# Weight chunks loaded one ahead, and a tile's loads issued before an older store, in a recurrent attention and FP4 feed-forward kernel

## The reference

```python
xn = layernorm(x)
# branch s: linear attention with phi(t) = exp(-t*t/2), 16 heads, then an MLP
q, k, v = rmsnorm(xn) @ qkv_w.T             # q, k -> phi(q), phi(k)
out = (phi(q) @ (phi(k).T @ v)) * z         # z: reciprocal of phi(q) @ sum(phi(k))
x2 = xn + gamma * (out @ proj_w.T + proj_b)
s = x2 + gamma * (gelu(rmsnorm(x2) @ conv1_w.T + conv1_b) @ conv2_w.T + conv2_b)
# branch g: feed-forward in which both operands of each product are quantized
gate = fq(xn) @ fq(w_gate).T                # w_gate, w_up: 2816 x 1024
up   = fq(xn) @ fq(w_up).T
h = silu(gate) * up
g = silu(fq(h) @ fq(w_down).T)              # w_down: 1024 x 2816
out = x + s * g
```

## Time and profile before

| | us |
|---|---|
| three runs | 7118.3, 7091.09, 7113.65 |
| their median | 7113.65 |
| the profiled execution | 7141.09 |
| its span on the slowest core (core 0) | 7139.5 |
| busy: VectorE (DVE) | 3880.3 |
| busy: TensorE matmul (PE) | 2700.8 |
| busy: ScalarE (ACT) | 2051.6 |
| busy: TensorE weight load (PEld) | 1144.1 |

### The profile page before, as it was taken

How to read it: one execution, slowest core, us unless ns; L and a number is a source line. 1 busy time by engine, 2 the same in 40 slices (tenths; PEclk the granted TensorE clock), 3 DMA queues, 4 the chain that set the end, 5 groups by cost and what they waited for, 6 DMA issues and landing times.

```text
span 7139.5 us, 58299 instructions; the slowest of 8 cores (7062.0 to 7139.5 us)
## 1 busy us (share of the span) xinstructions
PE 2700.8 (38%) x10905; PEld 1144.1 (16%) x11098; DVE 3880.3 (54%) x8760; ACT 2051.6 (29%) x4067; POOL 3.2 (0%) x13
## 2 busy tenths in 40 slices
PE   0066446643214033375003555522222322222299
PEld 0022122211101011132001222211111111111043
DVE  0500330033676866524886777667777777777522
ACT  0133223321222222221223333323333333333211
POOL 0000000000000000000000000000000000000000
PEclk9988678866556566677556667755555555555598
DMA  8500010013111110000113222221101110111254
GB/s 100 144 22 24 31 46 23 19 40 77 36 40 34 37 35 32 31 24 26 49 37 93 88 88 88 84 64 41 41 28 41 41 40 29 41 41 41 71 177 172
DMA packets 227699, 396.08 MB, mean 55 GB/s; under 512 B 147861, under 2 KB 147989, under 8 KB 217626
## 3 DMA queue, kind: packets, MB, share of 16 engines
q1 hardware_dynamic: 226778, 375.57, 16.2%
q0 software_dynamic: 576, 16.78, 2.1%
HBM read 246.44 MB, written 145.33 MB: 55 GB/s over the span
## 4 chain that ended last, share of the span: by engine, by line
PE 31%; issue 25%; DVE 20%; ACT 12%; DMA 6%; SPq 5%; DVEq 1%; ACTq 0%
PE ups L1121 5%; PE gps L1067 5%; PE kvg_ps L394 4%; PE d_ps L1219 4%; PE c1ps L911 3%; SPq L195 2%; PE c2ps L939 2%; DMA xqu<-xqT_h 2%; PE q_ps L443 2%; PE prA L588 2%; DVE gld L1133 1%; DMA winw<-L_ffn_w_up 1%; PE xp4t L1153 1%; DMA winw<-L_ffn_w_gate 1%; DMA xa<-x 1%
## 5 line engine op out<-in xcount | busy, mean ns | idle before, releaser
L1153 PE MATMUL xp4t<-ident_b,hq 128*128 128x128 bf16 x704 | 179.1, 262 | 1308.4 <-ACT hqf L1159 1259.9
L1121 PE MATMUL ups<-wquT,xqu 128*128 128x512 bf16 (+1 forms) x1504 | 381.8, 424 | 240.8 <-DMA xqu<-xqT_h 207.6
L363 DVE SCALAR_TENSOR_TENSOR xn<-xn,rstd_all,rep_s 128x1024 bf16<-128x1024 f32 x32 | 41.1, 1285 | 689.7 <-ACT xn L352 689.7
L1133 DVE TENSOR_TENSOR gld<-gld,up 128x2816 f32<-128x2816 f32 x32 | 98.9, 3092 | 562.0 <-ACT up L1130 562.0
L891 PE MATMUL xp2t<-ident_b,xn 128*128 128x128 bf16 x256 | 64.5, 265 | 875.2 <-DVE xn L879 664.0
L1067 PE MATMUL gps<-wqgT,xqf 128*128 128x512 bf16 (+1 forms) x1504 | 372.1, 416 | 31.6 <-ACT xqf L1056 31.6
L1049 PE MATMUL xp3t<-ident_b,xq 128*128 128x128 bf16 x256 | 67.8, 265 | 825.2 <-DVE xq L729 796.0
L1219 PE MATMUL d_ps<-wqdT,hln 128*128 128x512 bf16 x1379 | 334.2, 405 | 59.8 <-DMA hln<-hqT_h 51.9
L690 ACT ACTIVATE qb_sgn<-qb_u 128x704 f32<-128x704 f32 x128 | 101.1, 790 | 838.9 <-DVE qb_u L683 838.1
L394 PE MATMUL kvg_ps<-qkvT,fmsup 128*128 128x512 bf16 x992 | 302.6, 470 | 29.7 <-ACT fmsup L378 25.0
L911 PE MATMUL c1ps<-fm,conv1T 128*128 128x512 bf16 x1000 | 264.5, 431 | 104.5 <-ACT hddf L920 96.6
(11 more groups left out here) (243 smaller groups left out, 6743.2 us busy)
## 6 DMA issues: line engine op xcount, KB each, us to landing
xa<-x SPq DMA_DIRECT2D x160, 512.0 KB, 3.7
gate_h<-gate SPq DMA_DIRECT2D x32, 1408.0 KB, 5.7
gld<-gate_h SPq DMA_DIRECT2D x32, 1408.0 KB, 7.0
hqT_h<-hqf SPq DMA_DIRECT2D x32, 704.0 KB, 3.8
hln<-hqT_h SPq DMA_DIRECT2D x32, 704.0 KB, 5.4
out<-otl SPq DMA_DIRECT2D x32, 512.0 KB, 3.0
winw<-L_ffn_w_gate SPq DMA_DIRECT2D x22, 512.0 KB, 3.6
winw<-L_ffn_w_up SPq DMA_DIRECT2D x22, 512.0 KB, 3.9
```

What stands on the lines that cost most here:

```text
L1121: S.add("pe", lambda pe, b=b, ic=ic, cgo=cgo, cgw=cgw, cgi=cgi: pe.matmul(u_ps[cgi % 4][:, 0:cgw], xqu[b][:, P * ic:P * (ic + 1)], wquT[:, ...
L1133: S.add("v", lambda v, b=b: v.tensor_tensor(gld[b][:], gld[b][:], up_t[b][:], op.mult), waits=["a2_g%d" % t, "a2_ue%d_5" % t], inc="V", ev ...
L1153: S.add("pe", lambda pe, b=b, ic=ic: pe.transpose(xp4_ps[ic % 2], hq[b][:, P * ic:P * (ic + 1)], ident_b[:]), waits=tw, inc="PE", ev="a2_t ...
```

## The change

Two edits in the generator and two in the order of a2:

- `wq_chunk_gen` ends a round right after it has issued the load. `wq_pump_all` runs this first round of chunk u+1 before the rest of chunk u, so that the load of u+1 stands ahead of the store of u in SyncE's list. A chunk now has 31 rounds. The load of chunk u+2 still waits for the store of chunk u, which frees the buffers.
- In a2 the store of `hqf` is taken out of `a2_back` into `a2_store`, which is called two tiles later, behind the loads of that tile.
- The load of `gld` for tile t waits for the end of the quantization of tile t-2 (a2_q..._3) instead of its multiply (a2_h).

```diff
--- before.py
+++ after.py
@@ -752,6 +752,7 @@
                 waits=[S.gev("wq_done%d" % (ui - 2), "V")] +
                       (["wq_st%d" % (ui - 2)] if ui >= 2 else []) + list(extra_waits),
                 inc="WI%d" % slot, ev="wq_ld%d" % ui)
+            yield
             nun = width // uw
             if nun == 2:
                 gens = [quant_gen(qts[un], win_t[:, uw * un:uw * (un + 1)],
@@ -803,8 +804,20 @@
             yield
 
         def wq_pump_all(chunks):
-            for args in chunks:
-                for _ in wq_chunk_gen(*args):
+            gens = [wq_chunk_gen(*args) for args in chunks]
+            prev = None
+            for gn in gens:
+                try:
+                    next(gn)
+                except StopIteration:
+                    gn = None
+                yield
+                if prev is not None:
+                    for _ in prev:
+                        yield
+                prev = gn
+            if prev is not None:
+                for _ in prev:
                     yield
 
         S.mark("p1")
@@ -1107,7 +1120,7 @@
                     inc="XU%d" % b, ev="a2_xq%d" % t)
                 S.add("sy", lambda sy, t=t, b=b: sy.dma_start(
                     out=gld[b][:], in_=g["gate_h"][P * t:P * (t + 1), :]),
-                    waits=["a1_gst%d" % t, S.gev("a2_h%d" % (t - 2), "V")],
+                    waits=["a1_gst%d" % t, S.gev("a2_q%d_3" % (t - 2), "V")],
                     inc="GL%d" % b, ev="a2_g%d" % t)
                 for cgi, (cgo, cgw) in enumerate(CGS):
                     for ic in range(8):
@@ -1159,14 +1172,18 @@
                     S.add("sc", lambda sc, b=b, ic=ic: sc.copy(
                         hqf[b][:, P * ic:P * (ic + 1)], xp4_ps[ic % 2]),
                         waits=fw, inc="SC", ev="a2_fme%d_%d" % (t, ic))
-                S.add("sy", lambda sy, t=t, b=b: sy.dma_start(
-                    out=g["hqT_h"][P * t:P * (t + 1), :], in_=hqf[b][:]),
-                    waits=["a2_fme%d_21" % t], inc="SH%d" % b, ev="a2_hst%d" % t)
-
-            for t in range(NT + 1):
+
+            def a2_store(t):
+                S.add("sy", lambda sy, t=t: sy.dma_start(
+                    out=g["hqT_h"][P * t:P * (t + 1), :], in_=hqf[t % 2][:]),
+                    waits=["a2_fme%d_21" % t], inc="SH%d" % (t % 2), ev="a2_hst%d" % t)
+
+            for t in range(NT + 2):
                 if t < NT:
                     a2_front(t)
-                if t >= 1:
+                if t >= 2:
+                    a2_store(t - 2)
+                if 1 <= t <= NT:
                     a2_back(t - 1)
 
         S.mark("p3a2")
```

## The result

The changed kernel takes 6798.94 us in the median of 10 runs (6776.64 to 6836.06), against 7112.44 of the kernel before in 10 runs beside it: 313.5 us less, ratio 0.9559 with a 95% interval of 0.9533 to 0.9584. The forecast was 6835, with 6770 to 6900 as range and 279 us as gain.

A forecast was written before the change was run, and what follows sets the result against it. The prediction took three stages as chains through VectorE, which stands still behind late loads. Gains of 159 (a2), 55 (p25) and 65 us (p2) sum to 279, from 7113.65 to 6835 us, range 6770 to 6900.

The forecast's parts named there:

- The chain in a2: Up stage: the load of xqu lies on the only chain; issued earlier, it saves 30 x 5.3 = 159 us.
- another wait takes its place: Rival in a2: the load is early but ScalarE's copies or the gate load hold instead; 6994 us, chance 0.04.
- What is late next: still the matmul burst: Up stage after the change: VectorE still stands for the matmul burst, 11 us per tile instead of 16.3.
- The clock: a2's matmul bursts: still start at 0.50 (1.2 GHz), so the burst was taken as long as before.
- The rival at 80 us: Rival in a2: the burst starts at the higher clock, 80 us more gain over 30 tiles; 6755 us, chance 0.08.
- p25: Down weights: seven later load waits go, 56.6 us, the first load 1 us later; 55 us, bounds 48 and 57.
- p2: Gate and up weights: load stalls give way to shorter store stalls, gain 69 less 4 us net; 65 us.
- The new stall: p2: VectorE waits 2.5 us for the previous chunk's store at 40 boundaries, 100 us in all.
- The first chunk: p2: one of 38 load stalls, 4.58 us each, counted as the first chunk's and left; 169 of 174.1 us go.
- The alignment: p2: pump cuts near chunk boundaries delay x2b or s, 16 us in sum; new cuts hit xn less; 4 us net.
- The queue rival: Rival in p2: SyncE stands once per chunk with x2b and s behind, gain there 0; 6900 us, chance 0.06.
- The slower rival: Rival in a2 and p2: TensorE keeps 1.2 GHz in the bursts, 204 and 325 us more; 7364 us, chance 0.02.

The follow-up runs named there:

- e3_gld_late: The changed kernel with the load of gld behind the older store again, only xqu's ahead; a2 1922.4 us, four runs of 6800.38 to 6874.65 us, no ratio.
- f4_gap: The changed kernel with a2's matmul burst also waiting until the store of tile t-2 has landed; three runs of 6959.09 to 7079.78 us, no ratio.
- f1_30rounds: The changed kernel without the generator's extra round, so 30 rounds per chunk as before; p2 1467.5 us, ratio 0.9553 to the kernel before.
- f2_nostorewait: The changed kernel with the load of chunk u+2 not waiting for the store of chunk u; ratio 0.9491 to the kernel before, inconclusive in time.
- best2: The changed kernel with two result buffers in p2, chunk loads not waiting for the store, a2's copies of tile t-1 ahead of the signs; ratio 0.9032.

## Why the prediction was right

*The chain in a2.* Right: the load was on the only chain, it is hidden by a tile, and the burst follows the transposes. 5.13 us of the gap went, where 5.3 was taken, and e3_gld_late shows that it was xqu and not gld. (The 5.51 of the rows had 0.4 us of a missing first matmul in it.) The rival that another wait takes its place is out: TensorE's other wait in a2 is the same 33.0 us. "What is late next: still the matmul burst" holds too, 10.6 us against the 11 that was said.

*The clock.* "I therefore take the burst as long as before" is the term that was mis-sized: the burst became 0.77 us shorter (12.34 to 11.57), 23 us over 30 tiles, and with 30 x 5.13 = 154 this makes 177 of the 178 of a2. The rival at 80 us didn't come: the burst still starts at 1.2 GHz, as the rows of the gate stage had it. The forecast had asked only whether the burst starts at the higher clock, and not whether it gets there earlier. That it does is measured; why isn't, beyond the 0.6 of some 1.5 us at 1.2 GHz that f4_gap gives the gap.

*p25.* Right in both terms: seven waits gone, and the first load 8.87 instead of 8.37 us with a second one behind it, where 1 us and at most one load more had been allowed.

*p2.* The new stall was 92.5 / 41 = 2.26 us, not 2.5, since a store that lands without a load beside it takes 2.0 us and not 2.2: 100 us becomes 92.5. The first chunk was mis-read: the prediction left 4.58 us of the 174.1 for its stall, but it has none in either kernel, as its first operation follows xn at once, so that all 38 stalls went. The alignment had been priced at 4 us net. Before, core 0 waited:

```profile
DVE xn L879 <- ACT x2f L876: 130.0, 19, 45.5
...
DVE scc L948 <- DMA s_h<-s_t: 6.5, 2, 3.3
```

The waits for x2f went from these 130.0 to 129.2, and those for s from 6.5 to 12.2, 5 in sum. So 174.1 - 92.5 - 5 = 77, which is the 77 of the stage. (With the waits of core 4 before, one of the cores that the stage's length is taken from, it is 75.) The net hides two terms, and f1_30rounds shows their size: without the extra round the two waits come to 151.5 us, 15 more than before, and the new cuts give back 10 of it. The forecast had 16 and 12. So the 9 us that the extra round brought in f1_30rounds are part of the 77 and don't come on top.

*The sum.* The misses are 12 us in p2, 19 in a2 and 2 in p25, all the same way: they make 33 of the 34 us by which the gain exceeds the forecast, and none of them hides another.

*The queue rival* was half a mechanism: SyncE does stand for each store, which costs 12.5 us of waiting here by f2_nostorewait and 20 in p2 once VectorE doesn't stand for the store itself (best2 against two buffers alone), but it doesn't eat the gain.

*The slower rival* needed a clock that stays low; in each of 29 bursts on each of cores 0 to 3 of the changed kernel it rose within 5.7 us.

## What to carry to other kernels

In a program of in-order lists, look at each transfer for what stands ahead of it in its engine's list, and not only for what it waits for: here a load whose data and buffer were free for a tile stood behind a store that wasn't, and one swap was worth 178 us. After hiding a transfer, price the wait that is next in the same place (here the store of a single buffer) and what its landing holds up. And ask the same of compute engines: 22 copies behind sixteen sign operations of the next tile cost 315 us, as much as all the transfers of this change together.

## What the runs showed of the hardware

- How soon TensorE got 2.4 GHz in a burst differed with what went before, although the transposes ahead of it ran at 1.2 GHz throughout: 5.4 us into the burst in the mean behind 5.1 us of idling for xqu, 3.9 us directly behind transposes, 4.5 us behind 4.5 us of idling for a store, and 4.5 us too where that idling was 5.6 us. No run here shows what sets it.
- A 256 KB store landed 2.0 us after its issue alone and 2.2 us with a 512 KB load right behind it (medians); the 0.2 us are a tenth of the wait that hung on it.
